# Gated graph layer: four rounded passes of the candidate placed between w4's rounded and low passes

## The chip, the cores and the metric

The kernel runs on one core of one Trainium2 chip. The time is device microseconds of one execution; lower is better.

## The reference

An input x of 128 graphs x 64 nodes x 256 features goes through two residual blocks. Both begin with a layer norm and a ReLU.

```python
# block 1: linear attention masked by the adjacency
h   = relu(layernorm(x))
rel = adj.T * ((h Wq^T)(h Wk^T)^T);  rel = rel / norm(rel, axis=2)
x   = x + rel (h Wv^T)
# block 2: three steps of a gated graph network
h = relu(layernorm(x))
for _ in range(3):
    a = adj h                              # a_in = a_out, av = [a, a]
    z = sigmoid(av w3^T + b3 + h u3^T + bu3)
    r = sigmoid(av w4^T + b4 + h u3^T + bu3)
    c = tanh(av w5^T + b5 + (r*h) u5^T + bu5)
    h = (1 - z) h + z c
x = x + h
```

## The kernel before

**Tiles.** Tokens (graph x node) are worked on in 16 groups of 512. The state h of a group is held with features on partitions: two halves c of 128 features, 512 tokens each. Since both halves of `av` are the same, the two halves of w3, w4 and w5 are added once at the start.

**Rounded and low parts.** Products are made from 32-bit numbers split in two: `_hi` is the number rounded to the matmul format (a copy on ScalarE), `_lo` is the rest (a subtraction on VectorE). A linear map takes three passes for each of 2 x 2 blocks: W_hi x_hi, W_hi x_lo, W_lo x_hi, so 12 matmuls of 128x512. "Rounded passes" are the two with x_hi, "low passes" the one with x_lo.

**Windows.** TensorE's work is a hand-written sequence of windows, one for each state step of one group, two groups (sets s = 0 and 1) in turn. A round is the six windows k = 1, 2, 3, 4, 5 and 0 of the next pair. There are 7 such rounds, then 5 windows without attention. Window w = 0 stands alone at the start. In k = 2 and k = 4 TensorE also does the queries, values and scores of the attention for a coming group, in k = 3 and k = 5 its weighted sum.

**Order of TensorE in a window** (`window`, L675): `reset_gate_h` (u3 on h, 12 matmuls), `reset_gate_a` (w4 on a), `candidate_a` (w5 on a, 12), `update_gate` (wz on a, 12), attention if any, `candidate_rh` (u5 on r*h, 12), `adjacency` for the other set (64 small matmuls from `t_s` or a fresh h). In `reset_gate_a` (L618) 8 rounded passes come first, then a wait for `fea_taken`, which VectorE raises when both `a_lo` are written, then 4 low passes, each pair ending with `r_full`. wz is w3 - w4: z's sum is built on r's in the same PSUM bank, once ScalarE has read r (`r_ready`).

**PSUM.** `gate` holds r and then z, `cand` the candidate, `fea` the adjacency product, queries and scores, `tok` the values and the weighted sum. Each has one bank for each half o.

**Other engines**, each with its own fixed order in its own `window`. ScalarE (L895): h_hi, layer norm outputs in some windows, r_s (sigmoid, L864), hxT_hi in k = 2 and 4, rh_hi, z_s, t_s (from the state that came back through DRAM, L843), tanh (raises `c_ready`), then both `a_hi` (raise `a_hi_ready`). VectorE (L1225): new state (L1184, L990) with its turn and both `a_lo`, attention parts and statistics, rh (L1216), hxT_lo, rh_lo, h_lo, d_s. POOL: the powers rstd and rnorm, and copies. SyncE issues the DMAs that take the state and the normed input hx through DRAM and back to change their layout.

Of the kernel before, what the change touches and what calls it, by code (L numbers as in the profile page):

```python
# [32 lines left out]
def gated_graph_kernel(nc, x, adj, adj_t, wq, wk, wv_t, w3_t, b3, u3_t, bu3, w4_t, b4, w5_t, b5,  # L33
# [8 lines left out]
    C = D // P  # L42
# [22 lines left out]
    def use_in_round(name, i):  # L65
        if name in TOK_ROUND:
            return i * len(TOK_ROUND) + (len(TOK_START) + TOK_ROUND.index(name))
        return i * len(FEA_ROUND) + (len(FEA_START) + FEA_ROUND.index(name))
# [7 lines left out]
    with ctx:  # L76
        def sb(name, shape, dt=f32):
            return ctx.enter_context(nc.sbuf_tensor(name, shape, dt))

        def sem(name):  # L80
            return ctx.enter_context(nc.semaphore(name))
# [25 lines left out]
        a_hi = [sb(f"a_hi{s}", [P, C, T], f32r) for s in range(2)]  # L107
        a_lo = [sb(f"a_lo{s}", [P, C, T], f32r) for s in range(2)]
# [48 lines left out]
        gate = ctx.enter_context(nc.psum_tensor("gate", [P, C, T], f32))  # L157
        cand = ctx.enter_context(nc.psum_tensor("cand", [P, C, T], f32))
# [12 lines left out]
        def blocks(t):  # L171
# [12 lines left out]
        m_full, w_sum, w_hi_ready, w_lo_ready, bias_ready = (  # L184
            sem("m_full"), sem("w_sum"), sem("w_hi_ready"), sem("w_lo_ready"), sem("bias_ready"))
# [5 lines left out]
        norm_full, norm_taken = sem("norm_full"), sem("norm_taken")  # L191

        r_full, z_full, c_full = sem("r_full"), sem("z_full"), sem("c_full")
        r_ready, z_ready, c_ready = sem("r_ready"), sem("z_ready"), sem("c_ready")
# [6 lines left out]
        h_new_ready = sem("h_new_ready")  # L201
# [227 lines left out]
        def _(pe):  # L429
            def product(dst, lhs, rhs, start, stop):  # L430

                (l_hi, l_lo), (r_hi, r_lo) = lhs, rhs
                nc.tensor.matmul(dst, l_hi, r_hi, start=start, stop=False, skip_group_check=True)  # L433
                nc.tensor.matmul(dst, l_hi, r_lo, start=False, stop=False, skip_group_check=True)  # L434
                return nc.tensor.matmul(dst, l_lo, r_hi, start=False, stop=stop, skip_group_check=True)  # L435

            def one(dst, lhs, rhs, start=False, stop=False):
                return nc.tensor.matmul(dst, lhs, rhs, start=start, stop=stop, skip_group_check=True)  # L438

            def weight(n, c, o):  # L440
                return W_hi[n][:, c, o * P:(o + 1) * P], W_lo[n][:, c, o * P:(o + 1) * P]

            def linear(dst, n, o, hi, lo, start, stop):
                for c in range(C):
                    last = product(dst, weight(n, c, o), (hi[:, c, :], lo[:, c, :]),
                                   start and c == 0, stop and c == C - 1)
                return last
# [41 lines left out]
            def queries(g, n):  # L489
                pe.wait_ge(hxT_hi_ready, 2 * g + 2)  # L490
                pe.wait_ge(hxT_lo_ready, 2 * g - 2)
                for c in range(C):
                    fea_wait(n, c)
                    linear(fea[:, c, :], "m", c, hxT_hi, hxT_lo, True, True).then_inc(fea_full, 1)
# [64 lines left out]
            def weighted_sum(n_v, n_rel):  # L559
                tok_done(n_v)  # L560
                pe.wait_ge(fea_taken, 2 * n_rel + 2)
                for j in range(HQ):
                    for q in (j, j + HQ):
                        for e in range(2):
                            keys = key_half(q, e)
                            last = nc.tensor.matmul(tok[half(e), q, :], S[keys, q, keys], v_s[keys, q, :],
                                                    start=True, stop=True)
                last.then_inc(tok_full, 2)
# [43 lines left out]
            def reset_gate_h(w, s):  # L612
                pe.wait_ge(h_hi_ready, 2 * w + 2)
                for o in range(C):
                    pe.wait_ge(z_ready, 2 * w + (o - 1))
                    linear(gate[:, o, :], "u3", o, h_hi[s], h_lo[s], True, False)

            def reset_gate_a(w, s, n_a):  # L618
                pe.wait_ge(a_hi_ready, 2 * w + 2)
                for o in range(C):  # L620
                    for c in range(C):
                        w_hi, w_lo = weight("w4", c, o)
                        one(gate[:, o, :], w_hi, a_hi[s][:, c, :])
                        one(gate[:, o, :], w_lo, a_hi[s][:, c, :])
                pe.wait_ge(fea_taken, 2 * n_a + 2)
                for o in range(C):
                    for c in range(C):
                        last = one(gate[:, o, :], weight("w4", c, o)[0], a_lo[s][:, c, :], stop=c == C - 1)
                    last.then_inc(r_full, 1)

            def update_gate(w, s):

                if isinstance(w, int) and w == 0:
                    pe.wait_ge(w_lo_ready, 7)
                for o in range(C):
                    pe.wait_ge(r_ready, 2 * w + (o + 1))
                    linear(gate[:, o, :], "wz", o, a_hi[s], a_lo[s], False, True).then_inc(z_full, 1)

            def candidate_a(w, s, norm=None):
                if isinstance(w, int) and w == 0:  # L640
                    pe.wait_ge(w_lo_ready, 6)
                for o in range(C):
                    if not (isinstance(w, int) and w == 0):
                        pe.wait_ge(c_ready, 2 * w + (o - 1))
                    if o == 1 and norm is not None:
                        pe.wait_ge(norm_taken, norm)
                    linear(cand[:, o, :], "w5", o, a_hi[s], a_lo[s], True, False)

            def candidate_rh(w, s):
                if isinstance(w, int) and w == 0:  # L650
# [24 lines left out]
            def window(i, k, use, attention=True, new=True):  # L675
                w, s, o = 6 * i + k, k % 2, 1 - k % 2
                if attention and k == 3:
                    weighted_sum(use("v X"), use("rel X"))
                elif attention and k == 5:
                    weighted_sum(use("v Y"), use("rel Y"))  # L680
                if k == 0:
                    pe.wait_ge(h_lo_new, 4 * i + 2)
                elif k == 1:
                    pe.wait_ge(h_lo_new, 4 * i + 4)
                else:
                    pe.wait_ge(h_lo_ready, 8 * i + 2 * (k - 1))
                reset_gate_h(w, s)
                reset_gate_a(w, s, use("adj %d" % (k - 1)) if k > 1 else use_in_round("adj 0" if k else "adj 5", i - 1))
                candidate_a(w, s)
                update_gate(w, s)  # L690
                if attention and k == 2:
                    queries(2 * i + 2, use("q X"))
                    values(2 * i + 2, use("v X"))
                    scores_by_set(use("rel X"), use("q X"))
                elif attention and k == 4:
                    queries(2 * i + 3, use("q Y"))
                    values(2 * i + 3, use("v Y"))
                    scores_by_set(use("rel Y"), use("q Y"))
                if new:
                    candidate_rh(w, s)  # L700
                else:
                    candidate_rh_last()
                if k == 5:
                    if new:
                        pe.wait_ge(h0_plain, 2 * i + 1)
                        adjacency(h0[o], use("adj 5"))
                elif k == 0:
                    pe.wait_ge(h0_plain, 2 * i)
                    adjacency(h0[o], use("adj 0"))
                else:  # L710
                    adjacency(t_s, use("adj %d" % k), 8 * i + 2 * k - 1)
# [14 lines left out]
            n = use_in_start  # L726
# [19 lines left out]
            norms_start(1, n("norm 1"))  # L746
            weighted_sum_start(1, n("sum 1"))
            pe.wait_ge(w_lo_ready, 5)
            reset_gate_a(0, 0, n("adj first"))
            pe.wait_ge(h_new_ready, 2)  # L750
            candidate_a(0, 0)
            update_gate(0, 0)
            tok_done(n("sum 1"))
            transpose_new(1, 1, tokT, tok_full)
# [3 lines left out]
            for i in range(PAIRS - 1):  # L758
                for k in (1, 2, 3, 4, 5):
                    window(i, k, lambda name: use_in_round(name, i))  # L760
                window(i + 1, 0, lambda name: use_in_round(name, i))
            for k in (1, 2, 3, 4):
                window(PAIRS - 1, k, use_in_end, attention=False)
# [664 lines left out]
```

## Time and profile before

| | |
|---|---|
| Time, median of 3 runs | 882.19 us (879.82 to 882.44) |
| The profiled execution's own time | 881.74 us |
| Its span | 880.0 us |
| TensorE matmul busy | 863.4 us, 98%, 7356 matmuls |
| TensorE weight load busy | 706.8 us, 80% |
| VectorE busy | 743.9 us, 85% |
| ScalarE busy | 492.5 us, 56% |
| POOL busy | 124.4 us, 14% |
| Granted TensorE clock | 0.998 of full |
| Chain that ended last | TensorE 49%, VectorE 18%, issue 12%, DMA 11% |

The page gives busy time and instructions of each engine, then the span in slices, the DMA queues, the chain of work that ended last and the costliest groups. The span is from the first to the last instruction; the execution's own time is 1.74 us longer. Matmuls are pipelined, so a row of one matmul overlaps the next; the spacing of starts tells the rate.

### The profile page before, as it was taken

Reading aid. Unit: us, or ns where it says so; the run is one execution under the profiler, and the core shown is the slowest. Engines: PE = TensorE matmul, PEld = TensorE weight load, DVE = VectorE, ACT = ScalarE, POOL = GpSimd, SP = SyncE. Lnnn points to the kernel's source line nnn. Section 1 sums busy time; section 2 is a strip of 40 time slices with the busy share of each in tenths; the row PEclk is TensorE's granted clock in tenths of the full one; section 3 lists DMA queues with packets and bytes.
Section 4 is the critical chain, followed back from the end, with each engine's and each line's share of the span. In section 5 each row is a group of like instructions: output and inputs, shape, how many; then the busy total and the mean of one; then the engine's idle time right before and its main releaser. Section 6 shows DMA issues by size and latency. Waiting matters only on the chain.

```text
span 880.0 us, 19328 instructions
## 1 busy us (share of the span) xinstructions
PE 863.4 (98%) x7356; PEld 706.8 (80%) x7356; DVE 743.9 (85%) x1518; ACT 492.5 (56%) x881; POOL 124.4 (14%) x161
## 2 busy tenths in 40 slices
PE   8999999999999999999999999999999999999997
PEld 7868888787888878878788788888888788788885
DVE  5988889888898888888988788888889888898666
ACT  5565655656456564665645646456554556555553
POOL 1110112101131020310112101120111301121000
PEclk9999999999999999999999999999999999999999
DMA  6013323623344243451424614155232543234222
GB/s 187 24 50 121 97 96 114 189 83 105 110 141 156 66 137 104 145 168 49 144 72 145 190 51 143 49 168 168 83 110 75 176 134 97 97 114 127 73 72 96
DMA packets 88451, 99.53 MB, mean 113 GB/s; under 512 B 8640, under 2 KB 80576, under 8 KB 88384
## 3 DMA queue, kind: packets, MB, share of 16 engines
q1 hardware_dynamic: 88384, 98.50, 35.3%
q8 instruction: 58, 0.95, 0.4%
q14 instruction: 9, 0.07, 0.0%
HBM read 50.76 MB, written 47.71 MB: 112 GB/s over the span
## 4 chain that ended last, share of the span: by engine, by line
PE 49%; DVE 18%; issue 12%; DMA 11%; ACT 5%; SPq 3%; POOL 2%; DVEq 0%; ACTq 0%; POOLq 0%
PE cand L438 8%; PE gate L438 7%; PE gate L433 5%; PE gate L434 5%; PE gate L435 5%; PE fea L590 3%; DMA h_back<-h_trip 3%; DVE c_s L1184 3%; PE cand L433 3%; PE cand L434 3%; PE cand L435 3%; DMA hx_trip<-hx 2%; DVE a_lo L990 2%; SPq L252 2%; DMA h_trip<-h_turned 2%
## 5 line engine op out<-in xcount | busy, mean ns | idle before, releaser
L864 ACT ACTIVATE r_s<-gate,b_r 128x512 f32<-128x512 f32 x96 | 60.7, 684 | 89.2 <-PE gate L438 89.1
L770 ACT ACTIVATE h_hi<-h 128x512 fp32r<-128x512 f32 x92 | 57.0, 630 | 67.9 <-DVE h L990 46.1
L770 ACT ACTIVATE rh_hi<-rh 128x512 fp32r<-128x512 f32 x96 | 58.9, 632 | 47.4 <-DVE rh L1216 47.4
L378 POOL TENSOR_TENSOR rstd<-vare,minus_half 128x4 f32<-128x4 f32 x32 | 41.6, 1301 | 292.6 <-DVE vare L1024 292.6
L433 PE MATMUL gate<-h_hi,W_hi_u 128*128 128x512 f32 x192 | 80.1, 417 | 0.2 <-DVE h_lo L990 0.2
L877 ACT ACTIVATE z_s<-gate,b_z 128x512 f32<-128x512 f32 x96 | 62.9, 681 | 28.2 <-PE gate L435 28.2
L1216 DVE TENSOR_TENSOR rh<-r_s,h 128x512 f32<-128x512 f32 x96 | 67.4, 743 | 10.4 <-ACT r_s L864 9.9
L433 PE MATMUL gate<-a_hi,W_hi_wz 128*128 128x512 f32 x192 | 74.8, 390 | 0.6 <-DVE W_lo_wz L990 0.6
L434 PE MATMUL gate<-h_lo,W_hi_u 128*128 128x512 f32 x192 | 75.2, 392 | 0.0
L435 PE MATMUL gate<-h_hi,W_lo_u 128*128 128x512 f32 x192 | 75.1, 391 | 0.0
L438 PE MATMUL cand<-rh_hi,W_hi_u 128*128 128x512 f32 x188 | 74.9, 398 | 0.0
L435 PE MATMUL cand<-a_hi,W_lo_w 128*128 128x512 f32 x192 | 74.8, 389 | 0.0
L433 PE MATMUL cand<-a_hi,W_hi_w 128*128 128x512 f32 x192 | 74.8, 389 | 0.0
L434 PE MATMUL cand<-a_lo,W_hi_w 128*128 128x512 f32 x192 | 74.8, 389 | 0.0
L435 PE MATMUL gate<-a_hi,W_lo_wz 128*128 128x512 f32 x192 | 74.7, 389 | 0.0
L438 PE MATMUL gate<-a_hi,W_hi_w 128*128 128x512 f32 x192 | 74.7, 389 | 0.0
L434 PE MATMUL gate<-a_lo,W_hi_wz 128*128 128x512 f32 x192 | 74.7, 389 | 0.0
L438 PE MATMUL gate<-a_hi,W_lo_w 128*128 128x512 f32 x192 | 74.7, 389 | 0.0
L438 PE MATMUL cand<-rh_hi,W_lo_u 128*128 128x512 f32 x188 | 73.3, 390 | 0.0
L1179 DVE SCALAR_TENSOR_TENSOR d_s<-z_s,h 128x512 f32<-128x512 f32 x96 | 62.1, 684 | 13.0 <-ACT z_s L877 13.0
L1184 DVE TENSOR_TENSOR c_s<-z_s,c_s 128x512 f32<-128x512 f32 x94 | 62.7, 667 | 9.9 <-ACT c_s L890 9.9
L1201 DVE STREAM_TRANSPOSE h_turned<-h 128x512 f32<-128x512 f32 x94 | 66.4, 706 | 5.6
(160 smaller groups left out, 2034.2 us busy)
## 6 DMA issues: line engine op xcount, KB each, us to landing
h_back<-h_trip SPq DMA_DIRECT2D x216, 128.0 KB, 2.8
h_trip<-h_turned SPq DMA_DIRECT2D x40, 512.0 KB, 2.6
x_s<-x SPq DMA_DIRECT2D x15, 512.0 KB, 5.1
out<-o_s SPq DMA_DIRECT2D x15, 512.0 KB, 3.9
hx_back<-hx_trip SPq DMA_DIRECT2D x56, 128.0 KB, 2.8
h_trip<-h_blk SPq DMA_DIRECT2D x14, 512.0 KB, 3.2
hx_trip<-hx SPq DMA_DIRECT2D x14, 256.0 KB, 3.3
hx_trip<-hx SPq DMA_DIRECT2D x28, 128.0 KB, 3.2
```

The source lines that it names most:

```text
L378: nc.gpsimd.tensor_tensor(rstd[n][:], vare[n][:], minus_half[:], ALU.pow).then_inc(rstd_ready[n], 1)
L433: nc.tensor.matmul(dst, l_hi, r_hi, start=start, stop=False, skip_group_check=True)
L434: nc.tensor.matmul(dst, l_hi, r_lo, start=False, stop=False, skip_group_check=True)
L435: return nc.tensor.matmul(dst, l_lo, r_hi, start=False, stop=stop, skip_group_check=True)
L438: return nc.tensor.matmul(dst, lhs, rhs, start=start, stop=stop, skip_group_check=True)
L770: return nc.scalar.activation(dst, src, ACT.Copy)
L864: nc.scalar.activation(r_s[:, c, :], gate[:, c, :], ACT.Sigmoid, bias=b_r[:, c:c + 1]).then_inc(r_ready, 1)
L877: nc.scalar.activation(z_s[:, c, :], gate[:, c, :], ACT.Sigmoid, bias=b_z[:, c:c + 1]).then_inc(z_ready, 1)
L1179: nc.vector.scalar_tensor_tensor(d_s[:, c, :], z_s[:, c, :], 1.0, h[s][:, c, :], ALU.subtract, ALU.mult).then_inc(diff_ready, 1)
L1184: nc.vector.tensor_tensor(c_s[:, c, :], z_s[:, c, :], c_s[:, c, :], ALU.mult).then_inc(prod_ready, 1)
L1201: nc.vector.transpose(h_turned[:, :, :, c, :].rearrange("p a q f -> p q a f"), h[o][:, c, :]).then_inc(h_is_turned, 1)
L1216: nc.vector.tensor_tensor(rh[:, c, :], r_s[:, c, :], h[s][:, c, :], ALU.mult).then_inc(rh_ready, 1)
```

## The change

The candidate's four rounded passes for o = 0 (w5 on a_hi) are moved in front of the wait for `a_lo`, between w4's 8 rounded passes and its 4 low passes. The rest of the candidate on a follows w4's low passes, with rounded passes ahead of low ones in each half. The wait for the free bank cand 0 (`c_ready`, or at the start `h_new_ready` and w5's split) moves with the four passes. At the start the wait for `h_new_ready` thus stands ahead of w4's low passes.

```diff
-            def reset_gate_a(w, s, n_a):
+            def rounded_a(dst, n, s, o, start=False):
+                for c in range(C):
+                    w_hi, w_lo = weight(n, c, o)
+                    one(dst[:, o, :], w_hi, a_hi[s][:, c, :], start=start and c == 0)
+                    one(dst[:, o, :], w_lo, a_hi[s][:, c, :])
+
+            def low_a(dst, n, s, o, stop=False):
+                for c in range(C):
+                    last = one(dst[:, o, :], weight(n, c, o)[0], a_lo[s][:, c, :], stop=stop and c == C - 1)
+                return last
+
+            def gate_and_candidate_a(w, s, n_a, c_first=None):
                 pe.wait_ge(a_hi_ready, 2 * w + 2)
                 for o in range(C):
-                    for c in range(C):
-                        w_hi, w_lo = weight("w4", c, o)
-                        one(gate[:, o, :], w_hi, a_hi[s][:, c, :])
-                        one(gate[:, o, :], w_lo, a_hi[s][:, c, :])
+                    rounded_a(gate, "w4", s, o)
+                if c_first is not None:
+                    pe.wait_ge(*c_first)
+                if isinstance(w, int) and w == 0:
+                    pe.wait_ge(w_lo_ready, 6)
+                else:
+                    pe.wait_ge(c_ready, 2 * w - 1)
+                rounded_a(cand, "w5", s, 0, start=True)
                 pe.wait_ge(fea_taken, 2 * n_a + 2)
                 for o in range(C):
-                    for c in range(C):
-                        last = one(gate[:, o, :], weight("w4", c, o)[0], a_lo[s][:, c, :], stop=c == C - 1)
-                    last.then_inc(r_full, 1)
+                    low_a(gate, "w4", s, o, stop=True).then_inc(r_full, 1)
+                low_a(cand, "w5", s, 0)
+                if not (isinstance(w, int) and w == 0):
+                    pe.wait_ge(c_ready, 2 * w)
+                rounded_a(cand, "w5", s, 1, start=True)
+                low_a(cand, "w5", s, 1)
...
-            def candidate_a(w, s, norm=None):
-                if isinstance(w, int) and w == 0:
-                    pe.wait_ge(w_lo_ready, 6)
-                for o in range(C):
-                    if not (isinstance(w, int) and w == 0):
-                        pe.wait_ge(c_ready, 2 * w + (o - 1))
-                    if o == 1 and norm is not None:
-                        pe.wait_ge(norm_taken, norm)
-                    linear(cand[:, o, :], "w5", o, a_hi[s], a_lo[s], True, False)
...
-                reset_gate_a(w, s, use("adj %d" % (k - 1)) if k > 1 else use_in_round("adj 0" if k else "adj 5", i - 1))
-                candidate_a(w, s)
+                gate_and_candidate_a(w, s, use("adj %d" % (k - 1)) if k > 1 else
+                                     use_in_round("adj 0" if k else "adj 5", i - 1))
...
-            reset_gate_a(0, 0, n("adj first"))
-            pe.wait_ge(h_new_ready, 2)
-            candidate_a(0, 0)
+            gate_and_candidate_a(0, 0, n("adj first"), (h_new_ready, C))
```

## Rows read from the trace of the kernel before

**Rows 1.** Waits, whole span: engine, line, releaser, us in total, times, longest

```profile
PE gate L438 <- DVE a_lo L990: 2.8, 6, 0.7
...
PE fea L590 <- ACT t_s L770: 0.8, 4, 0.2
```

**Rows 2.** Timeline of TensorE: start us, us, instruction, count, idle before; k=3, k=4

```profile
308.57 1.07 PE L438 MATMUL gate<-a_lo,W_hi_w 128*128 128x512 f32 x4
309.47 0.39 PE L433 MATMUL cand<-a_hi,W_hi_w 128*128 128x512 f32 x1
...
324.20 1.20 PE L438 MATMUL gate<-a_lo,W_hi_w 128*128 128x512 f32 x4 [0.55 <-DVE a_lo L990]
```

**Rows 3.** Timeline of TensorE: w4's low passes in other windows

```profile
59.46 1.19 PE L438 MATMUL gate<-a_lo,W_hi_w 128*128 128x512 f32 x4 [0.32 <-DVE a_lo L990]
...
218.12 1.19 PE L438 MATMUL gate<-a_lo,W_hi_w 128*128 128x512 f32 x4
...
392.13 1.19 PE L438 MATMUL gate<-a_lo,W_hi_w 128*128 128x512 f32 x4
...
430.71 1.19 PE L438 MATMUL gate<-a_lo,W_hi_w 128*128 128x512 f32 x4 [0.67 <-DVE a_lo L990]
...
696.29 1.19 PE L438 MATMUL gate<-a_lo,W_hi_w 128*128 128x512 f32 x4 [0.27 <-DVE a_lo L990]
...
749.99 1.21 PE L438 MATMUL gate<-a_lo,W_hi_w 128*128 128x512 f32 x4 [0.37 <-DVE a_lo L990]
```

**Rows 4.** Timeline of VectorE, from k=2 to k=4 of the third round

```profile
288.31 1.31 DVE L1038 STREAM_TRANSPOSE hxT<-hx_back 128x512 f32<-128x512 f32 x2 [2.04 <-DMA hx_back<-hx_trip]
...
310.39 1.66 DVE L1118 SCALAR_TENSOR_TENSOR x_s<-tok,rnorm,x_s 128x256 f32<-128x256 f32 x4 [1.24 <-POOL rnorm L382]
...
322.87 1.28 DVE L990 TENSOR_TENSOR a_lo<-fea,a_hi 128x512 fp32r<-128x512 f32 x2
```

**Rows 5.** Timeline of VectorE and TensorE at the start (window 0)

```profile
38.51 1.29 DVE L1147 COPY h<-cand 128x512 f32<-128x512 f32 x2
...
40.74 1.07 PE L438 MATMUL gate<-a_lo,W_hi_w 128*128 128x512 f32 x4
```

**Rows 6.** Timelines from r to rh_hi: k=1 (four rows), k=3 (two rows)

```profile
377.52 1.27 ACT L864 ACTIVATE r_s<-gate,b_r 128x512 f32<-128x512 f32 x2 [1.36 <-PE gate L438]
380.60 1.29 DVE L1216 TENSOR_TENSOR rh<-r_s,h 128x512 f32<-128x512 f32 x2
381.33 1.23 ACT L770 ACTIVATE rh_hi<-rh 128x512 fp32r<-128x512 f32 x2 [2.54 <-DVE rh L1216]
383.22 0.39 PE L438 MATMUL cand<-rh_hi,W_hi_u 128*128 128x512 f32 x1
...
312.68 1.24 ACT L770 ACTIVATE rh_hi<-rh 128x512 fp32r<-128x512 f32 x2 [2.19 <-DVE rh L1216]
314.91 0.39 PE L438 MATMUL cand<-rh_hi,W_hi_u 128*128 128x512 f32 x1
```

**Rows 7.** Timeline of VectorE in k=0

```profile
363.38 1.71 DVE L1216 TENSOR_TENSOR rh<-r_s,h 128x512 f32<-128x512 f32 x2 [0.23 <-ACT r_s L864]
...
368.11 1.30 DVE L1038 STREAM_TRANSPOSE h<-h_back 128x512 f32<-128x512 f32 x2 [1.61 <-DMA h_back<-h_trip]
```

**Rows 8.** Timelines of VectorE and TensorE in k=4 of the third round

```profile
326.19 1.69 DVE L1216 TENSOR_TENSOR rh<-r_s,h 128x512 f32<-128x512 f32 x2 [0.24 <-ACT r_s L864]
327.81 1.48 DVE L990 TENSOR_TENSOR hxT_lo<-hxT,hxT_hi 128x512 fp32r<-128x512 f32 x2
330.68 0.39 PE L433 MATMUL fea<-hxT_hi,W_hi_m 128*128 128x512 f32 x1
...
335.03 0.69 DVE L1066 COPY v_s<-tok 128x512 f32<-128x512 f32 x1 [0.74 <-PE tok L435]
```

**Rows 9.** Timeline of TensorE: end of k=1, fourth round; queries in k=2, fifth round

```profile
386.34 1.16 PE L590 MATMUL fea<-adjT,t_s 64*64 64x64 f32 x64 [0.24 <-ACT t_s L770]
...
505.65 0.47 PE L433 MATMUL fea<-hxT_hi,W_hi_m 128*128 128x512 f32 x1 [0.47 <-issue]
```

## Prediction: what moving the four passes does to the time

> **What bounds the kernel now.** I read the page's busy shares first, then the waits, then the order of time of one round (about 106 us: windows k = 1 to 5 and 0). TensorE is busy 98% of the span and its clock is granted in full throughout, so only its gaps and its instruction count can move the time; the change keeps all 7356 matmuls. The waits view puts the longest steady waits of TensorE on `a_lo`, 2.8 us in 6 places, and on `t_s`, 0.8 us in 4 [rows 1]. Both are in the round; the other waits are one-offs at the start and the end.
>
> The idle figure of that view understates a stall. Four 128x512 matmuls take 309.47 - 308.57 = 0.90 us when nothing stops them, 0.226 us from start to start, while one row shows 0.39 us because neighbours overlap [rows 2]. A stall shown as 0.55 us therefore costs 0.55 + 0.39 - 0.23 = 0.71, and the group that restarts reads 1.20 us where an unstopped one reads 1.07: another 0.13 [rows 2]. Read so, every start of w4's low passes gives:
> - k = 4, seven windows: 0, 0.25, 0.72, 0.83, 0.76, 0.02 and 0.54 us, and the restart of 0.13 in five of them, about 0.07 in the other two; the second, fourth and seventh stand in [rows 3], the third in [rows 2].
> - k = 2: no idle time, but a restart in six of seven windows, 0.13 to 0.17 us each; one stands [rows 3].
> - k = 1: 0.48 + 0.13 in the first round, 0.14 in the second, 0.43 + 0.13 in the last; the first and the last stand [rows 3].
> - k = 3, 5 and 0, and the 5 windows at the end: none.
>
> By round, the first to the seventh, this is 0.7, 0.7, 1.0, 1.1, 1.0, 0.2 and 1.4 us, 6.1 us in all. That is the most the change can find.
>
> **Why `a_lo` is late in k = 4.** VectorE runs without waiting for TensorE from 288.31, where it waited for `hx_back`, through one wait of 1.24 us for POOL's `rnorm`, to the two `a_lo` of k = 4, which end at 322.87 + 1.28 = 324.15 [rows 4]. TensorE's first low pass starts 0.05 us behind that. So the time of `a_lo` there is set by VectorE's queue and not by TensorE: coming earlier buys nothing, other work to do meanwhile does.
>
> **The change, part by part.** (1) *Four rounded passes of w5, o = 0, go ahead of the wait for `a_lo`.* They are 4 x 0.226 = 0.91 us of work that needs only `a_hi` (same data as w4's rounded passes) and a free bank cand 0. Every stall above is under 0.91, so all are filled, restart included. (2) *The wait for `c_ready` 2w - 1 comes before them.* ScalarE issues both tanh of the last window ahead of both `a_hi`, so `a_hi_ready` implies it: cost nothing; if it ever were late, w4's low passes, r and everything after it would be queued behind it. (3) *The o = 1 half keeps its place*, in another order of passes: nothing, since the rows show the same 0.39 us and 0.226 us spacing for all three kinds of pass.
>
> (4) *At the start* the wait for `h_new_ready` and for w5's low part now stands ahead of w4's low passes. The two copies of h end at 38.51 + 1.29 = 39.80, w5's split before them, and TensorE gets there at 40.74 [rows 5]: covered by 0.94 us. `r_full` comes 0.91 later there, but VectorE reaches `rh` only four and a half microseconds after r_s. Nothing.
>
> (5) *`r_full` comes later* by 0.91 us minus the stall that was there, in all 48 windows, and the work between r_full and `candidate_rh` is shorter by as much. This is the price of the change, and it is paid where r -> rh -> rh_hi is tight:
> - k = 1: r_s (ScalarE) runs 377.52 to 378.79; VectorE is busy with statistics and begins rh at 380.60; rh_hi ends at 382.56, TensorE wants it at 383.22 [rows 6]. Moved by 0.91, r_s ends at 379.70, still 0.9 before rh. Nothing; without that cover the margin of 383.22 - 382.56 = 0.66 would be 0.25 short, 0.38 with a restart.
> - k = 3: the same shape. rh waits behind the attention's sum, which waits for rnorm [rows 4]; rh_hi ends at 313.92, TensorE comes at 314.91 [rows 6]. Nothing, and 0.99 of margin beside it.
> - k = 0: here VectorE does wait for r_s, 0.23 us; rh moves 0.9, and behind it in the queue stands the turn of h, which waits 1.61 us for its DMA [rows 7]. Covered by that 1.61; if the DMA were early, h_lo of the next window would take up to 0.9.
> - k = 4: VectorE waits 0.24 for r_s. `hxT_lo` ends at 327.81 + 1.48 = 329.29, the queries start at 330.68 [rows 8]. The margin of 1.39 falls to 0.48: nothing. Behind that VectorE waits 0.74 us for TensorE's values, twice; one stands [rows 8]. That is why the gain of k = 4 can be kept: TensorE is again the later one there, and VectorE can follow it by 0.7 us or more.
> - k = 2: r_s moves by 0.8, but `hxT` stands ahead of rh on VectorE. Nothing. The windows at the end have little on VectorE and more than a microsecond of margin.
>
> **What is next, and what comes back.** Gains before k = 4 can't add to the gain in k = 4: `a_lo` there keeps its time, so a round gives at most the 0.91 us of work put ahead (third and fourth: 0.91 each). In k = 1 the next wait is `t_s` [rows 9], which follows from VectorE's and ScalarE's queues; it stalled TensorE 0.24 in the fourth round and also in the second and the last, so the k = 1 gains of those are given back. In one k = 2 the queries already wait for hx [rows 9]: the 0.15 of the fifth round is lost. In the first, the queries' margin of about 0.3 lets half of 0.7 through. Kept: 0.3 + 0.55 + 0.91 + 0.91 + 0.88 + 0.2 + 0.83 = 4.6 us.
>
> Sum against the profiled execution: span 880.0 - 4.6 = 875.4, and with the 1.74 us around it 877.1 for 881.74. The median shown is 0.45 above that execution: 882.19 - 4.6 = 877.6.
>
> The price of a restart is where a page can be held against a row. The rows give 0.13 us. The Trainium skill (TensorE: Matmul & The Clock Gate, "Single matmul latency" and "Back-to-back issue gap") says that a matmul that stands alone pays its drain, (398 + 512)/2.4 = 379 ns against 215.7 ns in a stream, an estimate of 0.163 per restart; over the roughly 14 restarts found here that would make 0.5 us more of gain. The same page's 215.7 ns does not agree with the 0.226 us of this trace, so I stay with the rows.
>
> **Rivals.**
> - *Handed back.* The gained time turns into waits for t_s (k = 1), hx (k = 2) or VectorE elsewhere. For: VectorE is busy 85% of the span and in k = 1 to 4 waits for little but DMA and POOL; those waits already show at TensorE in some rounds [rows 9], and DMA landings shift from run to run. Against: the two waits of 0.74 and the 1.61 for the DMA in k = 4 and k = 0. All handed back gives 882.2; half, 882.2 - 2.3 = 879.9.
> - *Slower: the late `r_full` reaches VectorE's queue.* In k = 4 and k = 0 VectorE waits for r_s today, and everything behind rh (the low parts, d_s, the new state, its DMA) moves with it. If the whole 0.91 us came through to TensorE there, 14 windows x 0.91 = 12.7 us, less 4.6: 882.2 + 8.1 = 890.3. It decides once the lateness exceeds the cover: 1.61 in k = 0, 1.39 to the queries in k = 4 [rows 7, 8]. Both hold by 0.5 us or more, which speaks against it; that a round is periodic and its DMA waits are not constant speaks for it.
> - *It doesn't do what it says.* The passes go ahead, but the wait is for something that moves with TensorE, so the stall only shifts by 0.91 us. Then the time is 882.2 as well. VectorE's row of 36 us without a wait for TensorE speaks against it.
>
> **How the numbers follow.** A measurement of this kernel can tell about 0.3%, 2.6 us, from no change. Forecast 877.6 us: chance 0.62, own range 875.8 to 879.5 (upper bound of gain 6.1, and 2.7 if k = 4 alone and only half of the rest counts). Handed back in half or in full, or no effect: 0.31, 879.9 to 882.2. Slower: 0.07. Faster by over 0.3% (below 879.5) 0.63, within 0.3% 0.30, slower 0.07. The range takes in the handed-back cases with the spread of the runs shown, 879.8 to 882.4, and leaves out the slower one: 875.4 to 882.9.
>
> **What would show it.** In the profile after, the wait for a_lo at TensorE should be gone or under 0.2 us in all, with w4's low groups at 1.07 us; r_s in k = 0 and k = 4 about 0.9 us nearer to update_gate; rh in k = 1 and k = 3 where it was; a wait for t_s in k = 1 not over 0.4 us in a round; the two waits for values in k = 4 shorter. Wrong if the t_s or hx waits grow by some 0.9 us a round (handed back), or if TensorE waits at `candidate_rh`, at update_gate for r_s, or at the queries in k = 4 (slower).

## The result

The changed kernel takes 877.13 us (median of 8, 875.74 to 878.68) where the kernel before takes 881.87 (879.06 to 884.92). The ratio is 0.994 with a 95% interval of 0.9925 to 0.9955: 0.45 to 0.75% faster. The forecast was 877.6. In a later session on one chip the changed kernel gave 876.9 and the kernel before 882.99, ratio 0.993 (0.9911 to 0.9949).

| | before | after |
|---|---|---|
| the profiled execution's own time | 881.74 us | 877.4 us |
| its span | 880.0 us | 875.6 us |
| TensorE matmul busy, count | 863.4 us, 7356 | 862.2 us, 7356 |
| VectorE busy | 743.9 us | 743.3 us |

The work is the same: the page counts as many instructions on every engine as before. The page's summary of the chain that ended last says where the time went:

```profile
PE 84%; DVE 5%; ACT 4%; issue 4%; DMA 2%; POOL 1%; SPq 1%; DVEq 0%; ACTq 0%; POOLq 0%
```

Before, TensorE held 49% of that chain, VectorE 18% and DMA 11%. Now it is nearly all TensorE: it runs from one instruction to the next and is rarely released by another engine. The share alone proves nothing, since it also moves between executions: in the profile of experiment 1, a kernel that is no faster than before, TensorE holds 66%. The waits of TensorE over the whole span, after (compare [rows 1]):

```profile
PE tok L578 <- DVE h L996: 2.3, 2, 1.3
PE cand L724 <- POOL ident L373: 2.2, 1, 2.2
PE fea L590 <- ACT t_s L776: 1.9, 4, 0.7
```

The wait for `a_lo` is not in the list at all. The first two lines are the end and the start of the kernel; the wait for `t_s` has grown from 0.8 to 1.9 us. The place of [rows 2] in the profile after, TensorE's timeline in k = 4 of the third round:

```profile
324.46 0.39 PE L438 MATMUL gate<-a_hi,W_lo_w 128*128 128x512 f32 x1
324.69 0.39 PE L438 MATMUL cand<-a_hi,W_hi_w 128*128 128x512 f32 x1
...
325.37 0.39 PE L438 MATMUL cand<-a_hi,W_lo_w 128*128 128x512 f32 x1
325.59 1.07 PE L438 MATMUL gate<-a_lo,W_hi_w 128*128 128x512 f32 x4
326.50 0.61 PE L438 MATMUL cand<-a_lo,W_hi_w 128*128 128x512 f32 x2
```

and VectorE's, which answers the last of [rows 4]:

```profile
323.86 1.28 DVE L996 TENSOR_TENSOR a_lo<-fea,a_hi 128x512 fp32r<-128x512 f32 x2
```

`a_lo` ends at 325.14 (323.86 + 1.28), 0.45 us after TensorE is done starting w4's rounded passes: without the fill it would have stood still until then. Instead the four passes of w5 start from 324.69 on, the low passes follow at 325.59 without a gap, and they have their unstopped length of 1.07 us.

**By round.** The start of `reset_gate_h` can be compared window by window in the two profiles. TensorE's lead over the kernel before grew, in the seven rounds, by 0.61, 0.10, 0.72, 1.08, 1.59, 0.30 and 0.57 us, 4.97 in all. The single windows show it plainly: from start to start, k = 4 of the fourth round took 23.65 us before and 22.71 after; the windows k = 5 and 0 behind it took 14.91 and 14.92 in both.

These are differences of two single executions. Against a second profile of the changed kernel (span 874.8 us) they are 0.21, 0.43, 0.95, 1.07, 1.79, 0.07 and 0.25, 4.8 in all. And from the start of the first round to the end of the seventh, experiment 1 below, which fills nothing, took 742.0 us where the kernel before took 743.7. So single rounds are good to some 0.3 us, and their sum to one or two.

**The start of this profile was slow for another reason.** The changed kernel comes to its first `reset_gate_h` 1.82 us later than the kernel before (35.81 against 33.99), before any changed instruction. Busy time by stretch from 24.0 to 27.2 us, the column PEclk being the granted clock as a share of 2.4 GHz, first before and then after:

```profile
24.00:27.20 3.20, 3.20 (x19) 2.71 (x18) 3.17 (x9) 0.98 (x2) 0.00 (x0) 1.00 0.01 3
```

```profile
24.00:27.20 3.20, 3.20 (x11) 2.62 (x11) 3.17 (x9) 1.19 (x2) 0.00 (x0) 0.50 0.01 3
```

At 0.50 (1.2 GHz) the 128x512 matmuls there start 0.43 us apart, not 0.23. From 20 to 24 us TensorE had been busy for 2.78 of 4 us, in both profiles. Ahead of the stretch the changed kernel was 0.23 us behind (the matmul after the wait for `S_hi` starts at 22.18 against 21.95), and behind it 1.81 (the values' matmuls start at 28.64 against 26.83), so the lower clock cost about 1.6 us here. The second profile of the changed kernel had 1.00 in this stretch, and of the profiles of the experiments those of 1, 5, 8 and the first of 9 had 0.53 to 0.55, the others 1.00. The fall comes in some executions and not in others, and it is no part of the change. It is not all that varies there: the second profile reaches its first `reset_gate_h` at 34.83, still 0.84 later than the kernel before.

**The end gave something too.** The 5 windows without attention take 59.68 us from start to start in both profiles, but from the last `reset_gate_h` to the end of the span there are 22.3 us before and 21.1 after. The last write of the state to DRAM is issued 4.87 us after that start before, and 3.95 after. Together: -1.8 at the start, 5.0 in the rounds and 1.2 at the end make the 4.4 us between the spans. In experiments 1 and 2, where w5's passes of the last windows stand behind w4's low passes as in the kernel before, the end takes 22.0 and 22.1 us; in all others it takes 21.1 to 21.5, also in experiment 4, where no wait is filled. So this microsecond goes with the order in the last windows and not with a filled wait. No run isolates it.

### The profile page after: what moved, and what is told of

Read it like the earlier page. It is cut to its first block, busy times and chain, and to the rows that moved or that the text cites. A ratio compares the mean times of both kernels' runs of the same rounds, so it can differ in the third digit from the quotient of the medians.

```text
span 875.6 us, 19328 instructions
## 1 busy us (share of the span) xinstructions
PE 862.2 (98%) x7356; PEld 709.4 (81%) x7356; DVE 743.3 (85%) x1518; ACT 491.0 (56%) x881; POOL 117.1 (13%) x161
## 4 chain that ended last, share of the span: by engine, by line
PE 84%; DVE 5%; ACT 4%; issue 4%; DMA 2%; POOL 1%; SPq 1%; DVEq 0%; ACTq 0%; POOLq 0%
PE cand L438 26%; PE gate L438 13%; PE gate L433 9%; PE gate L434 9%; PE gate L435 9%; PE fea L590 6%; PE fea L523 2%; PE tok L433 2%; PE tok L434 2%; PE tok L435 2%; PE fea L433 2%; PE fea L435 1%; PE fea L434 1%; PE tok L566 1%; DMA h_back<-h_trip 1%
## 5 line engine op out<-in xcount | busy, mean ns | idle before, releaser
L1222 DVE TENSOR_TENSOR rh<-r_s,h 128x512 f32<-128x512 f32 x96 | 64.9, 715 | 22.8 <-ACT r_s L870 22.3
L996 DVE TENSOR_TENSOR h<-c_s,d_s 128x512 f32<-128x512 f32 (+1 forms) x98 | 66.8, 681 | 3.4
```

Source lines behind the costliest of these rows:

```text
L996: return nc.vector.tensor_tensor(dst, a, b, ALU.subtract)
L1222: nc.vector.tensor_tensor(rh[:, c, :], r_s[:, c, :], h[s][:, c, :], ALU.mult).then_inc(rh_ready, 1)
```

## The experiments

All were run beside the kernel before on one chip in each session; its medians in the three sessions were 882.05, 881.58 and 882.99. The edits are against the changed kernel and in short form: where passes move, the wait for their free bank moves with them, and what a condition spares keeps the changed kernel's order unless the text says otherwise. Two questions: does the gain come from filling the wait, and what does the late `r_full` cost?

**1. The new order of passes alone.** The four passes stay behind w4's low passes.

```diff
-                rounded_a(cand, "w5", s, 0, start=True)
                 pe.wait_ge(fea_taken, 2 * n_a + 2)
                 for o in range(C):
                     low_a(gate, "w4", s, o, stop=True).then_inc(r_full, 1)
+                rounded_a(cand, "w5", s, 0, start=True)
```

> All of the candidate's passes stay behind w4's low passes, as in the kernel before; only their order is the new one (rounded, then low, in each half). Fill theory (the gain comes from work done during the wait for a_lo): 882, as before, with the wait for a_lo at TensorE back at about 2.8 us. Rival, the new order of the passes is itself cheaper: 877.3, as the changed kernel.

Measured: 881.49, ratio 0.9995 (0.9975 to 1.0014). TensorE's waits:

```profile
PE gate L438 <- DVE a_lo L996: 1.7, 3, 1.0
PE fea L590 <- ACT t_s L776: 1.0, 4, 0.3
```

The wait for `a_lo` is back and the gain is gone. The order of the passes is worth nothing that these runs can tell: the interval reaches from 2.2 us faster to 1.2 slower.

The wait is smaller than the 2.8 us expected, and it lies elsewhere. 1.05 us of it is in k = 1 of the seventh round, and of the k = 4 windows only that of the third round shows one (0.3 us). That is a matter of when the DMA of hx lands. VectorE's turn of `hxT`, from which it runs on to the `a_lo` of k = 4, begins 5.9 to 7.1 us after the start of k = 2 in this execution and 6.1 to 8.0 in that of the kernel before. So how long k = 4 stalls changes from one execution to the next.

**2. Only k = 4 filled.** The other windows keep the order of experiment 1.

```diff
-                rounded_a(cand, "w5", s, 0, start=True)
+                if k == 4:
+                    rounded_a(cand, "w5", s, 0, start=True)
                 pe.wait_ge(fea_taken, 2 * n_a + 2)
                 for o in range(C):
                     low_a(gate, "w4", s, o, stop=True).then_inc(r_full, 1)
+                if k != 4:
+                    rounded_a(cand, "w5", s, 0, start=True)
```

> The four passes go ahead of the wait in the seven windows k = 4 alone. Fill theory: the stalls of k = 4 (3.1 us) and their restarts (0.8) go, 882 - 3.9 = 878.1. If the gain came evenly from all windows: 7/48 of 4.7, 881.3.

Measured: 877.97, ratio 0.995 (0.9934 to 0.9966), 4.1 us of the gain out of 7 windows of 48. The a_lo wait that is left, 1.3 us in 2 places, lies in k = 1 of the first and the last round. The fill theory's 878.1 holds, and it is k = 4 that carries the change. The microsecond at the end is not in it: it takes 22.1 us here.

**3. Two passes ahead in place of four**, 0.45 us of work.

```diff
-                rounded_a(cand, "w5", s, 0, start=True)
+                w_hi, w_lo = weight("w5", 0, 0)
+                one(cand[:, 0, :], w_hi, a_hi[s][:, 0, :], start=True)
+                one(cand[:, 0, :], w_lo, a_hi[s][:, 0, :])
                 pe.wait_ge(fea_taken, 2 * n_a + 2)
                 for o in range(C):
                     low_a(gate, "w4", s, o, stop=True).then_inc(r_full, 1)
+                w_hi, w_lo = weight("w5", 1, 0)
+                one(cand[:, 0, :], w_hi, a_hi[s][:, 1, :])
+                one(cand[:, 0, :], w_lo, a_hi[s][:, 1, :])
```

> Only two of the four rounded passes of w5 go ahead of the wait (0.45 us), the other two come behind w4's low passes. Fill theory: of the k = 4 stalls 0.27 to 0.38 us stay in three rounds and 0.1 in a fourth, with their restarts, about 1.5 us; k = 1 and k = 2 are filled: 877.3 + 1.5 = 878.8, a wait for a_lo of about 0.5 to 1 us in all. If any fill at all were enough: 877.3. If the gain went with the amount of work put ahead: 879.7.

Measured: 877.63, ratio 0.9956 (0.9939 to 0.9973).

```profile
PE fea L590 <- ACT t_s L781: 1.3, 3, 0.6
...
PE gate L438 <- DVE a_lo L1001: 0.6, 2, 0.3
```

0.6 us of the wait is left, as reckoned, but the time lies closer to the changed kernel than the 878.8 expected. The runs do not separate 877.6 from 877.1; they do show that the first half of the fill brings most of the gain.

**4. The lateness alone.** The wait comes first, so nothing is filled, but `r_full` is 0.91 us later in every window.

```diff
-                rounded_a(cand, "w5", s, 0, start=True)
                 pe.wait_ge(fea_taken, 2 * n_a + 2)
+                rounded_a(cand, "w5", s, 0, start=True)
                 for o in range(C):
                     low_a(gate, "w4", s, o, stop=True).then_inc(r_full, 1)
```

> The wait for a_lo comes first, then w5's four rounded passes, then w4's low passes: nothing fills the wait, but r_full is 0.91 us later in all 48 windows. If that lateness is covered as reckoned (0.25 of slack or more in every window): 882, within 0.5 us. If it costs what the gain of the changed kernel falls short of all stalls and restarts (6.1 - 4.7): 883.4. If it reaches VectorE's queue in k = 4 and k = 0 in full: 894.7.

Measured: 883.79, ratio 1.0023 (1.0004 to 1.0043), so between 0.4 and 3.8 us slower than before. It is near the middle one of the three numbers and far from 894.7; the lower end of the interval is within the 0.5 us of the first. The profile doesn't show a single place for it, and it is of an execution of 880.71 us, 3 us under the median. In it the wait for `a_lo` was 3.0 us in 6 places, and single windows were up to 0.9 us shorter and up to 1.5 us longer than in the kernel before.

**5. The lateness doubled.** As experiment 4 with all eight rounded passes of w5 behind the wait: 1.81 us.

> The wait for a_lo first, then w5's eight rounded passes, then w4's low passes: no stall is filled, r_full is 1.81 us later. By what eight ahead cost against four (2.9 us, seen as a wait of 0.72 us for t_s in k = 1 of each round): 882 + 2.9 = 884.9, partly taken up by the a_lo waits, so 883.5 to 885, with waits for t_s at TensorE of 0.7 us. If the lateness is free and the cost of eight ahead came from something else: 882.

Measured: 889.75, ratio 1.0084 (1.006 to 1.0107). That is 8 us slower, and more than either theory said.

```profile
PE cand L438 <- DVE a_lo L996: 4.0, 9, 0.6
...
PE fea L590 <- ACT t_s L776: 1.4, 6, 0.2
```

The t_s waits are short, 0.2 and not 0.7. What grew is the wait for `a_lo`, and in windows that had none before: from start to start, k = 0 takes 15.23 and 15.20 us and k = 1 15.52 and 15.50 us in the fourth and fifth rounds, where the kernel before had 14.92 and 14.92, 15.25 and 15.14. A late r makes the next `a_lo` late, and with nothing ahead of the wait TensorE pays for it at once. I had reckoned with t_s only. Part of the 8 us in the profile is something else: one wait of 1.7 us before the queries in k = 2 of the seventh round.

**6. Eight passes ahead of the wait.** The wait is filled as in the changed kernel, and `r_full` is 1.81 us later.

```diff
                 rounded_a(cand, "w5", s, 0, start=True)
+                pe.wait_ge(c_ready, 2 * w)
+                rounded_a(cand, "w5", s, 1, start=True)
                 pe.wait_ge(fea_taken, 2 * n_a + 2)
```

> All eight rounded passes of w5 go ahead of the wait for a_lo, r_full is 1.81 us later. No stall is over 0.91, so nothing more is filled. By the margins of the kernel before, the queries of k = 4 have 1.39 - 1.81 = -0.42 us and a restart of 0.13: 7 x 0.55 = 3.9 us, so 877.3 + 3.9 = 881.2, with a wait for hxT_lo at TensorE in k = 4. If lateness costs nothing at all: 877.3. If it costs in all windows by what it exceeds 0.91: 48 x 0.9 = 43 us, 920.

Measured: 879.97, ratio 0.9977 (0.9961 to 0.9992), 2.8 us slower than the changed kernel by its first result. The size came near the forecast of 881.2, and the place was wrong: no wait at the queries of k = 4, but one for t_s in k = 1 of every round from the second on. Beside it there are two waits in k = 1 of the seventh round, 0.9 us for `h_lo` and 0.6 us for `rh_hi` at `candidate_rh`.

```profile
PE fea L590 <- ACT t_s L776: 4.3, 6, 0.7
```

VectorE's timeline in k = 5 and k = 0 tells how it gets there (the second line answers the first of [rows 7]):

```profile
350.37 1.29 DVE L1222 TENSOR_TENSOR rh<-r_s,h 128x512 f32<-128x512 f32 x2 [0.56 <-ACT r_s L870]
...
365.36 2.18 DVE L1222 TENSOR_TENSOR rh<-r_s,h 128x512 f32<-128x512 f32 x2 [1.39 <-ACT r_s L870]
...
368.84 1.30 DVE L1044 STREAM_TRANSPOSE h<-h_back 128x512 f32<-128x512 f32 x2
```

In k = 5 rh now waits 0.56 us for r_s, where it did not wait before. In k = 0 it waits 1.39, and the turn of h behind it has no wait for its DMA left: VectorE's own queue is the later one. From that turn VectorE works without a pause to the rh of k = 1, and t_s follows from it.

**7. Eight ahead, but four in k = 0.**

```diff
                 rounded_a(cand, "w5", s, 0, start=True)
+                if k != 0:
+                    pe.wait_ge(c_ready, 2 * w)
+                    rounded_a(cand, "w5", s, 1, start=True)
                 pe.wait_ge(fea_taken, 2 * n_a + 2)
```

> As eight ahead, but in k = 0 four ahead as in the changed kernel. Theory: what eight ahead costs comes through k = 0 alone, where the late r holds rh and behind it the turn of the next state of h on VectorE, which then has no wait for its DMA left; here that cover is back, so 877.3 with waits for t_s as in the changed kernel. Rival, the lateness costs in each window a little (k = 1 itself, or the queries in k = 4): 880, with 0.7 us waits for t_s in k = 1.

Measured: 879.58, ratio 0.9974 (0.9961 to 0.9987). The theory fell: k = 0 alone does not carry the price.

```profile
PE fea L590 <- ACT t_s L793: 4.0, 7, 0.7
```

VectorE's turn of h in k = 0:

```profile
368.87 1.31 DVE L1061 STREAM_TRANSPOSE h<-h_back 128x512 f32<-128x512 f32 x2 [1.32 <-DMA h_back<-h_trip]
```

Now VectorE is early and waits 1.32 us for the DMA, but that DMA lands later. Counted from the start of k = 5 the turn begins at 26.05 to 26.65 us in six of seven rounds, against 25.4 to 25.9 in six of seven of the kernel before. The DMA queue shows why. SyncE's timeline in the third round, first of the kernel before (k = 5 starts at 342.35), then of this one (342.71):

```profile
362.00 0.34 SPq L285 DMA_DIRECT2D h_trip_last<-h_turned  x1
363.11 1.79 SPq L252 DMA_DIRECT2D h_back<-h_trip  x4
```

```profile
363.02 0.34 SPq L285 DMA_DIRECT2D h_trip_last<-h_turned  x1
363.47 2.20 SPq L252 DMA_DIRECT2D h_back<-h_trip  x4
```

The write of the old group's turned state goes out 20.31 us after the start of k = 5 and not 19.65, since VectorE's late rh of k = 5 pushes everything behind it. So it stands 0.45 us ahead of the four reads of the new h in place of 1.11. The first read is issued at 20.76 in both, but the four together take 2.20 us to issue in place of 1.79, and the last of them lands at 26.13 in place of 25.73. From the second round on this is the same in every round of both kernels with eight passes ahead in k = 5, and in no round of the kernel before or of the changed one. That the write and the reads hinder each other is inferred from these times.

**8. Eight ahead, but four in k = 5 and k = 0.** 

```diff
-                if k != 0:
+                if k not in (5, 0):
```

> Eight ahead, but four in k = 5 and in k = 0. In the two kernels with eight ahead in k = 5, VectorE's rh waited 0.56 us for r_s there, where it did not wait before, and the DMA that brings back the new h landed about 0.5 us later. Theory: the price of eight ahead comes through k = 5 and k = 0 together, so here it is gone: 877.1, waits for t_s under 0.4 us in most rounds. Rival, it comes through k = 1 itself or k = 2 to 4: 879.6, as with k = 0 alone spared, and 0.6 us waits for t_s.

Measured: 876.73, ratio 0.9922 (0.9901 to 0.9943), beside 876.9 for the changed kernel in the same session.

```profile
PE fea L590 <- ACT t_s L793: 0.9, 2, 0.7
```

VectorE's turn of h in k = 0 of this kernel:

```profile
367.75 1.31 DVE L1061 STREAM_TRANSPOSE h<-h_back 128x512 f32<-128x512 f32 x2 [0.19 <-DMA h_back<-h_trip]
```

The price is gone, and with it most t_s waits. So within the spread of these runs, about 2 us, 1.81 us of lateness is free in k = 1, 2, 3 and 4 and costs in k = 5 with k = 0. The state's write is issued at 19.66 us after the start of k = 5 again, and the four reads take 1.77 us to issue. The layer norm's output that the reads bring back was written at the same time in all profiles compared (16.02 to 18.10 us after the start of k = 5), so it isn't the new h that is late. A kernel with k = 5 alone spared was not run: since sparing k = 0 alone brought nothing, k = 5 may carry the whole price.

**9. t_s ahead of z in k = 1**, on top of the change, to take away the wait that is left.

```diff
-                if k == 3:
+                if k in (1, 3):
                     take_back(w)
                     update_sigmoid(w)
```

> The changed kernel, and in k = 1 ScalarE copies t_s ahead of its two z sigmoids, as it does in k = 3. t_s is the wait that is left: 1.9 us in 4 places in the profile of the changed kernel, and restarts of 0.13. If h has come back from DRAM by then, t_s ends 1.2 us earlier and these waits go: 877.3 - 2.2 = 875.1. Rival: z, 1.1 us later, holds d_s and the new state on VectorE, and a_lo of k = 2 comes late; the four passes ahead cover 0.91 of that, the rest shows as a wait for a_lo: 877.3 or up to 1.5 more.

> The changed kernel with t_s copied ahead of the z sigmoids in k = 1, once more, now beside the changed kernel on the same chip. If the waits for t_s were time lost: 1.9 us and four restarts under the changed kernel, 875.0. If its first result was luck: as the changed kernel, 877.1.

The changed kernel beside the second of them:

> The changed kernel once more, beside the two below on the same chip: 877.1 by its first result; by the stalls counted in the kernel before, 877.6.

Measured: t_s first 874.95, ratio 0.9921 (0.9901 to 0.994), and again 876.26, ratio 0.9922 (0.9903 to 0.9941); the changed kernel beside the second 876.9, ratio 0.993 (0.9911 to 0.9949). In both profiles of t_s first no wait for t_s is listed. In the fourth round of the second ScalarE's timeline reads

```profile
383.23 1.14 ACT L776 ACTIVATE t_s<-h_back 128x512 f32<-128x512 f32 x2
384.27 1.24 ACT L883 ACTIVATE z_s<-gate,b_z 128x512 f32<-128x512 f32 x2
```

and TensorE's

```profile
384.70 1.16 PE L590 MATMUL fea<-adjT,t_s 64*64 64x64 f32 x64
```

The wait is removed as meant, and no new wait for `a_lo` is listed. But most of it comes back at the next place, the queries of k = 2, which wait for hx. TensorE in the fourth round of the same profile (compare the second of [rows 9]):

```profile
397.31 0.47 PE L433 MATMUL fea<-hxT_hi,W_hi_m 128*128 128x512 f32 x1 [0.34 <-issue]
```

Summed over the seven rounds, k = 1 takes 105.3 us here and 107.1 in the first profile of the changed kernel, 1.8 less; k = 2 takes 161.1 and 159.5, 1.6 more. In the other profile of t_s first it is 2.0 less and 1.2 more. So a wait listed as 1.9 us was worth far less than the 2.2 expected. Beside the changed kernel the difference is 0.6 us, and the ranges overlap (875.72 to 877.12 and 876.54 to 878.01). Against the kernel before it is 0.6 to 1.0% faster in each of its two sessions, as is experiment 8 with the same ratio in one; that it beats the changed kernel is not shown.

## Why the prediction was right, point by point

**What bounds the kernel.** Right. TensorE's gaps were all there was to win, and the count of matmuls did not move.

**How much was there.** The stalls and restarts summed to 6.1 us, of which 4.6 were to be kept; 4.7 came. Experiments 1, 2 and 4 show that the fill is the mechanism: with the new order alone nothing, with the lateness alone a loss, with k = 4 alone 4.1 us against 3.9 reckoned. That the sum fits to 0.1 us is luck. The rounds gave 5.0 and 4.8 in the two profiles, the end 1.2 that the forecast had no term for, and the medians of the kernel before differ by up to 1.4 us between sessions. The lower end of the forecast's own range, 875.8, doesn't follow from its 6.1 us either (882.19 - 6.1 = 876.1).

**What a round can keep.** The sum is right, its parts are not. Forecast 0.3, 0.55, 0.91, 0.91, 0.88, 0.2 and 0.83; measured 0.61, 0.10, 0.72, 1.08, 1.59, 0.30 and 0.57. The step that failed is the cap of 0.91 us. I took VectorE's stretch before k = 4 as fixed in time, but it begins with a DMA, and that DMA follows from earlier work of TensorE. The write of hx to DRAM is issued 2.88 us before k = 2 starts in six of seven rounds of the kernel before, and 2.88 to 2.97 us in six of the changed one. From the turn of `hxT` to the end of the `a_lo` of k = 4 VectorE needs 35.84 to 35.86 us in five of seven rounds before (36.83 at most) and 35.83 to 35.85 in six after. So the length of the stretch is fixed and its start is not. (The stretch is read too simply as well: beside the wait for `rnorm` it has one of 1.33 us for ScalarE's `sq` at 302.08 and one of 0.30 us for `rstd` at 319.27, neither of them for TensorE.)

In the fourth round, k = 2 gave 0.15 and k = 4 gave 0.94 after it. In the fifth, the wait at t_s was gone and the stall at the queries [rows 9] fell from 0.63 us to 0.26, where I had them eat a gain. This second part is not the change's doing: experiment 1 fills nothing and has no stall at these queries, the second profile of the changed kernel has none either, and the landing of that DMA differs between executions. In the second round a longer wait did the opposite:

```profile
175.81 1.16 PE L590 MATMUL fea<-adjT,t_s 64*64 64x64 f32 x64 [0.61 <-ACT t_s L776]
281.33 1.16 PE L590 MATMUL fea<-adjT,t_s 64*64 64x64 f32 x64 [0.26 <-ACT t_s L776]
386.71 1.16 PE L590 MATMUL fea<-adjT,t_s 64*64 64x64 f32 x64 [0.27 <-ACT t_s L776]
...
703.63 1.16 PE L590 MATMUL fea<-adjT,t_s 64*64 64x64 f32 x64 [0.71 <-ACT t_s L776]
```

This is TensorE's timeline after, at the end of k = 1 (compare the first of [rows 9]). The wait was forecast to stay under 0.4 us in a round and reached 0.61 and 0.71; in the second profile it was 0.51 and 0.71 in the same two rounds.

**Handed back.** A part of this rival is real: 1.9 - 0.8 = 1.1 us more wait for t_s. It is a share of what was won. Experiment 9 takes it out of k = 1, but most of it comes back in k = 2, so for what is left the rival's mechanism holds.

**The price of a late r.** Right for 0.91 us, and each cover named was there. VectorE in k = 0, after (compare [rows 7]):

```profile
364.64 1.30 DVE L1222 TENSOR_TENSOR rh<-r_s,h 128x512 f32<-128x512 f32 x2 [1.12 <-ACT r_s L870]
366.04 1.95 DVE L996 TENSOR_TENSOR rh_lo<-rh,rh_hi 128x512 fp32r<-128x512 f32 x2
368.48 1.30 DVE L1044 STREAM_TRANSPOSE h<-h_back 128x512 f32<-128x512 f32 x2 [0.49 <-DMA h_back<-h_trip]
```

The wait for r_s grew by 0.89 us and the wait for the DMA behind it fell by 1.12: the cover took it, with 0.49 left. In k = 1 rh stands 8.4 us after the start of its window in both profiles of the fourth round, and rh_hi's margin is as it was. In k = 4 hxT_lo ends at 330.28 and the queries start at 331.03: the margin of 1.39 us fell to 0.75, where 0.48 was reckoned. VectorE there (compare [rows 8]):

```profile
327.19 1.69 DVE L1222 TENSOR_TENSOR rh<-r_s,h 128x512 f32<-128x512 f32 x2 [0.24 <-ACT r_s L870]
328.80 1.48 DVE L996 TENSOR_TENSOR hxT_lo<-hxT,hxT_hi 128x512 fp32r<-128x512 f32 x2
...
335.39 0.69 DVE L1072 COPY v_s<-tok 128x512 f32<-128x512 f32 x1 [0.30 <-PE tok L435]
336.82 0.69 DVE L1072 COPY v_s<-tok 128x512 f32<-128x512 f32 x1 [0.75 <-PE tok L435]
```

The first wait for the values fell from 0.74 to 0.30 and the second stayed: VectorE has room to follow TensorE, as forecast.

**What the margins missed.** The list of covers had no figure for k = 5, and that is a place where more lateness is paid. There, in the kernel before, rh begins 7.2 us after the window and the first r_s is there at 6.0: 1.2 us of cover, enough for 0.91 and not for 1.81 (experiment 6). The slower rival had the right mechanism in that the late r reaches VectorE's queue, and the wrong place and point: not the queries of k = 4, whose r_s was held by ScalarE's layer norm anyway, but k = 5 and k = 0. It decides between 0.91 and 1.81 us of lateness. Experiments 4 and 5 add that the lateness is not free where the wait isn't filled: alone, 0.91 us of it cost 0.4 to 3.8 us and 1.81 us cost 8.

## What to carry to other kernels

When an in-order engine waits for an operand, put ahead of the wait as much independent work as the longest stall lasts, and no more: here the first 0.45 us brought most of the gain, 0.91 us all of it, and 1.81 us gave more than half of it back, unless the two windows with the least cover were spared. Work put ahead makes a result later in every window, not only in those that stalled, so list the cover of each kind of window and look for the smallest. A stall is the gap in the starts plus the longer restart behind it; the idle column alone showed 2.8 of the 6.1 us.

## What the runs showed of the hardware

The granted clock stood at its 1.2 GHz level from 24.0 to 27.2 us of one execution of the changed kernel (0.50 in the stretch shown above) and at 2.4 GHz in another execution of the same kernel. It made about 1.6 of the 1.82 us by which the first `reset_gate_h` of the profile shown stands behind that of the kernel before, though no changed instruction had run. Five of the thirteen profiles of this case have such a stretch there. Whoever compares two profiles should look for it, and compare start, rounds and end each by itself, before explaining the rest.
